# One load of x per sequence in place of two: three input tiles that become the result, the norm's four pieces and the bias add spread out, and the transposes of the sum put ahead of those of the heads

## The reference

```python
qk = x @ W_attn + b_attn                  # q, k; the values are x itself
y = _causal_attn(q, k, v)                 # first attention
e = v[:, :, 1:, :] - y[:, :, :-1, :]
k2 = x[:, :-1] @ W_k2 + b_k2
y2 = _causal_attn(q2, k2, e)              # second attention, on e
...
return proj(y) + proj(y2)                 # = (y + y2) @ W_proj + 2 b_proj
...
x = _layernorm(x + attn(x))               # for every sequence
x = _layernorm(x + ffn(x))                # ffn touches sequence 0 alone
```

## Time and profile before

| | |
|---|---|
| time, median of 3 runs | 2399.45 us (2398.83 to 2400.66) |
| the profiled execution's own time | 2397.73 us |
| its span in the profile | 2395.9 us |
| TensorE busy | 2311.0 us, 96% |
| VectorE / ScalarE / GpSimd busy | 2076.4 (87%) / 1788.7 (75%) / 1552.9 us (65%) |
| granted TensorE clock, mean | 0.987 |
| DMA, mean | 105 GB/s, queues busy 54.3% |
| HBM read / written | 74.60 MB / 16.78 MB |

### The profile page before, as it was taken

One profiled execution on the slowest core, in us unless ns is written; L12 is line 12 of the kernel. 1 busy time (PEld: TensorE's weight loads), 2 busy tenths in 40 slices (PEclk: granted clock), 3 DMA queues, 4 the chain that ended last, 5 costly groups with the idle time before them and its releaser, 6 DMA issues.

```text
span 2395.9 us, 64955 instructions
## 1 busy us (share of the span) xinstructions
PE 2311.0 (96%) x19670; PEld 1324.6 (55%) x19670; DVE 2076.4 (87%) x9178; ACT 1788.7 (75%) x3456; POOL 1552.9 (65%) x2439
## 2 busy tenths in 40 slices
PE   6999999999999999999999999999999999999997
PEld 4555555555555555555555555555555555555454
DVE  5889998998998989989998899998988999998555
ACT  3677777787877777777777787877777777777653
POOL 4466666766766676676666766766676676666432
PEclk9799999999999999999999999999999999999999
DMA  7455555655656556565655656555565565655111
GB/s 122 90 109 109 104 96 101 122 114 114 113 104 109 96 112 119 110 119 109 113 95 99 124 113 114 113 104 109 99 109 116 111 120 109 112 97 89 55 56 59
DMA packets 187749, 250.83 MB, mean 105 GB/s; under 512 B 26760, under 2 KB 103184, under 8 KB 187408
## 3 DMA queue, kind: packets, MB, share of 16 engines
q1 hardware_dynamic: 186448, 245.10, 54.3%
q10 hardware_dynamic: 960, 1.57, 0.5%
HBM read 74.60 MB, written 16.78 MB: 38 GB/s over the span
## 4 chain that ended last, share of the span: by engine, by line
PE 71%; ACT 12%; POOL 6%; issue 5%; DMA 2%; SPq 2%; DVE 1%; ACTq 0%; POOLq 0%; DVEq 0%
PE out_t L668 21%; PE score_t L707 18%; PE misc L759 10%; PE score L718 8%; PE out_t L733 6%; ACT heads_t L589 5%; ACT prob L563 5%; PE misc L801 4%; POOL prob L451 2%; PE score L859 2%; SPq L385 2%; DMA stack_q<-neg_l 2%; ACT resid L287 1%; PE misc L785 1%; PE score L875 1%
## 5 line engine op out<-in xcount | busy, mean ns | idle before, releaser
L923 DVE CUSTOM_DVE_ANT_0 junk<-score,mask_rows 128x384 bf16<-128x384 f32 (+3 forms) x3584 | 1682.2, 515 | 227.5 <-PE score L718 219.1
L563 ACT ACTIVATE prob<-score_t 128x512 f32<-128x512 f32 x2560 | 1368.5, 599 | 262.9 <-PE score_t L707 261.1
L451 POOL TENSOR_SCALAR_AFFINE_SELECT prob<-prob 128x512 f32<-128x512 f32 (+1 forms) x1280 | 712.3, 561 | 648.2 <-ACT prob L563 638.4
L707 PE MATMUL score_t<-stack_q,stack_k 50*128 50x128 f32 (+5 forms) x4096 | 982.2, 359 | 19.7 <-DMA stack_q<-neg_l 6.7
L718 PE MATMUL score<-stack_k,stack_q 48*128 48x512 f32 (+3 forms) x4096 | 982.0, 348 | 2.7 <-DVE max_cols L923 1.2
L707 PEld LDWEIGHTS score_t<-stack_q,stack_k 50*128 50x128 f32 (+1 forms) x4096 | 611.5, 186 | 556.5 <-ACT prob L563 304.8
L668 PE MATMUL out_t<-prob,value 128*17 128x512 f32 (+3 forms) x8192 | 657.4, 439 | 0.0
L718 PEld LDWEIGHTS score<-stack_k,stack_q 48*128 48x128 f32 x4096 | 618.1, 188 | 24.5 <-DVE max_cols L923 9.7
L923 DVE DVE_READ_ACCUMULATOR2_ANT max_cols<- 128x1 f32 x4096 | 339.5, 83 | 0.0
L668 PEld LDWEIGHTS out_t<-prob,value 128*17 128x17 f32 x8192 | 184.5, 97 | 211.7 <-issue 130.7
L479 POOL TENSOR_TENSOR part_l<-part_f,part_h 128x512 fp32r<-128x512 f32 x192 | 245.7, 1280 | 16.3
(11 more groups left out here) (100 smaller groups left out, 1727.0 us busy)
## 6 DMA issues: line engine op xcount, KB each, us to landing
stack_k<-part_h SPq DMA_DIRECT2D x512, 128.0 KB, 4.6
stack_k<-part_l SPq DMA_DIRECT2D x256, 128.0 KB, 5.1
stack_q<-part_h SPq DMA_DIRECT2D x248, 128.0 KB, 4.2
x_full<-x_turned SPq DMA_DIRECT2D x32, 512.0 KB, 13.0
x_in<-L_attn_x SPq DMA_DIRECT2D x32, 512.0 KB, 14.8
resid<-L_attn_x SPq DMA_DIRECT2D x32, 512.0 KB, 5.2
stack_q<-part_l SPq DMA_DIRECT2D x124, 128.0 KB, 5.1
layer_out<-resid SPq DMA_DIRECT2D x31, 512.0 KB, 7.9
```

The source lines that it names most:

```text
L451: e.affine_select(out=view, in_=view, compare_op=ALU.is_ge, fill=0.0, base=-unit_parts(unit)[1], pattern=[[0, runs], [0, cut], [1, P]], ch ...
L563: e.activation(prob[pair % RING][:, slot % 2 * 512:slot % 2 * 512 + 512], score_t[time % KEY_DEPTH][:, :], ACT.Exp, scale=1.0 / np.sqrt(HE ...
L707: done = e.matmul(score_t[now % KEY_DEPTH][:, col:col + n], keys[rows, pair, kb * P:(kb + 1) * P], stack_q[b % 2][rows, pair, kb * P:token ...
L923: e.tensor_tensor_reduce(junk[count % JUNK][:, 0:n], score[number % MAX_DEPTH][:, col:col + n], mask, 1.0, -3e38, ALU.add, ALU.max, max_co ...
```

## The change

x is loaded once, into `x_in[b % 3]`, at (5,5) of the sequence before (SP waits there for the store that last read this tile). The copy into `value1` moves from (5,2) to (7,2). The tile stays, takes the bias in two halves at (4,4) and (7,6) of its own sequence, then the projection, is normed in place and is stored from there. The load of `resid` at (2,2) with its wait is gone. The four pieces of the norm go from (0,7), (0,9), (1,1), (1,3) to (0,8), (3,1), (3,6), (4,4), and the store from (1,5) to (4,7). Sequence 0 is now stored like the others and read back into `x1_routed`, which lies over `x_full`. On PE the block that turns `y_sum` stands ahead of the transposes of the heads.

```diff
 USUAL = {"proj": ((3, 7), (6, 7)), "added": ((4, 0), (7, 0)), "stats": ((5, 5), (6, 4), (7, 5), (8, 1)),
-         "var": ((8, 3),), "guess": ((8, 4),), "refine": ((8, 5),), "apply": ((8, 7), (8, 9), (9, 1), (9, 3)), "store": ((9, 5),)}
+         "var": ((8, 3),), "guess": ((8, 4),), "refine": ((8, 5),), "apply": ((8, 8), (11, 1), (11, 6), (12, 4)), "store": ((12, 7),)}
...
-        x_in = sb("x_in", [P, blocks, width])
+        x_in = [sb(f"x_in{i}", [P, blocks, width]) for i in range(3)]
         x_next = sb("x_next", [P, blocks, width])
-        resid = sb("resid", [P, blocks, width])
...
+        x_full_at = nc.sbuf_base
         x_full = sb("x_full", [P, halves, tokens])
...
+        x1_routed = nc.alloc_sbuf_tensor_at("x1_routed", [P, blocks, width], F32, offset=x_full_at)
...
-                    if b + 1 < batches:
-                        e.wait_ge(s_value1, b + 1)
-                        e.dma_start(x_in[:, :, :], x[b + 1].rearrange("(t p) c -> p t c", p=P)).then_inc(s_x, 16)
...
-                b = ahead - 1
-                if (place, slot) == (2, 2) and 0 <= b < batches:
-                    if b == 1:
-                        e.wait_ge(s_apply, blocks)
-                    elif b > 1:
-                        e.wait_ge(s_out, 16 * (b - 1))
-                    e.dma_start(resid[:, :, :], x[b].rearrange("(t p) c -> p t c", p=P)).then_inc(s_resid, 16)
...
+                b = ahead + 1
+                if (place, slot) == (5, 5) and 2 <= b < batches:
+                    if b >= 3:
+                        e.wait_ge(s_out, 16 * (b - 2))
+                    e.dma_start(x_in[b % 3][:, :, :], x[b].rearrange("(t p) c -> p t c", p=P)).then_inc(s_x, 16)
...
+                if time == SLOTS * (last_batch + 1):
+                    e.wait_ge(s_xsplit, 2 * halves * batches)
+                    e.wait_ge(s_out, 16)
+                    e.dma_start(x1_routed[:, :, :], out[0].rearrange("(t p) c -> p t c", p=P)).then_inc(s_x1, 16)
...
-                if (place, slot) == (3, 6) and 0 <= ahead - 1 < batches:
-                    wide = bass.AP(bias2[:, :].tensor, bias2[:, :].offset, [list(bias2[:, :].ap[0]), [0, blocks], [1, width]])
...
-                    e.tensor_tensor(resid[:, :, :], resid[:, :, :], wide, ALU.add).then_inc(s_biased, 1)
+                for half in range(2):
+                    if (place, slot) == ((4, 4), (7, 6))[half] and 0 <= ahead < batches:
+                        rows2 = x_in[ahead % 3][:, 2 * half:2 * half + 2, :]
...
+                        e.tensor_tensor(rows2, rows2, wide, ALU.add).then_inc(s_biased, 1)
...
-                if (place, slot) == (5, 2) and 0 <= ahead + 1 < batches:
+                if (place, slot) == (7, 2) and 0 <= ahead + 1 < batches:
...
-                    apply_norm(e, b, t, x1_routed if b == 0 else resid, resid)
+                    apply_norm(e, b, t, x_in[b % 3], x_in[b % 3])
...
+                b = ahead - 1
+                if 0 <= b < batches:
+                    for hf in range(halves):
+                        if (place, slot) == ((1, 4), (2, 4))[hf]:
+                            e.wait_ge(s_full, min(N_PIECES * (b + 2) + 2 + hf, N_PIECES * batches))
+                            if hf == 0:
+                                e.wait_ge(s_added, GROUPS * (b + 1))
+                            else:
+                                e.wait_ge(s_yt, halves * b + 1)
+                            for t in range(blocks):
+                                done = e.transpose(misc[:, t * P:(t + 1) * P], y_sum[b % 2][:, t, hf * P:(hf + 1) * P], ident[:, :])
+                            done.then_inc(s_yt_pe, 1)
+
+
                 if slot == 4 and 0 <= unit - 1 < end:
                     e.wait_ge(s_heads, unit)
```

More of the change, by code:

```diff
@@ L150, in build_layer @@
         misc = ps("misc", 512)
-        s_wq, s_wk2, s_wproj, s_next, s_resid, s_out = (sem(f"s_{n}") for n in ("wq", "wk2", "wproj", "next", "resid", "out"))
-        s_x, s_xt = sem("s_x"), sem("s_xt")
+        s_wq, s_wk2, s_wproj, s_next, s_out = (sem(f"s_{n}") for n in ("wq", "wk2", "wproj", "next", "out"))
+        s_x, s_xt, s_x1 = sem("s_x"), sem("s_xt"), sem("s_x1")
         s_stack = {(kind, hf): sem(f"s_stack_{kind}{hf}") for kind in ("q", "k", "k2") for hf in range(halves)}
@@ L372, in _ @@
                     if piece[3] == N_PIECES // 3:
-                        e.dma_start(x_in[:, :, :], x[0].rearrange("(t p) c -> p t c", p=P)).then_inc(s_x, 16)
+                        e.dma_start(x_in[0][:, :, :], x[0].rearrange("(t p) c -> p t c", p=P)).then_inc(s_x, 16)
                         e.dma_start(wp[:, :, :], w_proj.rearrange("(h p) n -> p h n", p=P)).then_inc(s_wproj, 16)
                         e.dma_start(bias2[:, :], b_proj.rearrange("(o n) -> o n", o=1).to_broadcast([P, width])).then_inc(s_wproj, 16)
+                if piece and piece[3] == N_PIECES:
+                    e.dma_start(x_in[1][:, :, :], x[1].rearrange("(t p) c -> p t c", p=P)).then_inc(s_x, 16)
+                b = ahead + 1
[3 more added lines that the diff above has]
+                    e.dma_start(x_in[b % 3][:, :, :], x[b].rearrange("(t p) c -> p t c", p=P)).then_inc(s_x, 16)
                 for a, b in ((0, ahead + 1), (1, ahead)):
@@ L388, in _ @@
                 now_due = due("store", time)
-                if now_due and now_due[0]:
+                if now_due:
                     b = now_due[0]
                     e.wait_ge(s_apply, blocks * (b + 1))
-                    e.dma_start(out[b].rearrange("(t p) c -> p t c", p=P), resid[:, :, :]).then_inc(s_out, 16)
+                    e.dma_start(out[b].rearrange("(t p) c -> p t c", p=P), x_in[b % 3][:, :, :]).then_inc(s_out, 16)
+                if time == SLOTS * (last_batch + 1):
+                    e.wait_ge(s_xsplit, 2 * halves * batches)
+                    e.wait_ge(s_out, 16)
+                    e.dma_start(x1_routed[:, :, :], out[0].rearrange("(t p) c -> p t c", p=P)).then_inc(s_x1, 16)
                 if step_at.get(time) == LOADS:
@@ L452, in _ @@
                                     pattern=[[0, runs], [0, cut], [1, P]], channel_multiplier=-1).then_inc(s_mask, 1)
[L454 to L459 removed]
+                for half in range(2):
+                    if (place, slot) == ((4, 4), (7, 6))[half] and 0 <= ahead < batches:
+                        rows2 = x_in[ahead % 3][:, 2 * half:2 * half + 2, :]
+                        wide = bass.AP(bias2[:, :].tensor, bias2[:, :].offset, [list(bias2[:, :].ap[0]), [0, 2], [1, width]])
+                        e.wait_ge(s_value1, ahead + 1)
+                        if ahead == 0:
+                            e.wait_ge(s_bias, 1)
+                        e.tensor_tensor(rows2, rows2, wide, ALU.add).then_inc(s_biased, 1)
                 for a, b in ((0, ahead + 1), (1, ahead)):
@@ L503, in _ @@
                     e.tensor_copy(value1[:, :, :, 0:HEAD_DIM],
-                                  x_in[:, :, :].rearrange("p t (h d) -> p t h d", d=HEAD_DIM)).then_inc(s_value1, 1)
+                                  x_in[b % 3][:, :, :].rearrange("p t (h d) -> p t h d", d=HEAD_DIM)).then_inc(s_value1, 1)
                 done = unit - 2
@@ L773, in _ @@
                                     ident[:, :]).then_inc(s_neg_pe, 1)
[L775 to L786, removed]
                 now_due = due("proj", time)
@@ L947, in _ @@
                     b, pair = now_due
-                    rows2 = resid[:, 2 * pair:2 * pair + 2, :]
+                    rows2 = x_in[b % 3][:, 2 * pair:2 * pair + 2, :]
                     e.wait_ge(s_proj, 2 * b + pair + 1)
-                    if pair == 0:
-                        e.wait_ge(s_biased, b + 1)
+                    e.wait_ge(s_biased, 2 * b + pair + 1)
                     e.tensor_tensor(rows2, misc[:, :].rearrange("p (t c) -> p t c", t=2), rows2, ALU.add).then_inc(s_attended, 1)
@@ L957, in _ @@
                         e.wait_ge(s_attended, 2 * b + t // 2 + 1)
-                    take_stats(e, b, t, resid)
+                    take_stats(e, b, t, x_in[b % 3])
                     if t == last:
```

5 lines of the change are left out of this document (2 added, 3 removed).

## The result

The changed kernel takes 2382.23 us (median of 5 runs, 2375.94 to 2386.96) against a median of 2399.45. The ratio on record is 0.9942, with a 95% interval of 0.9925 to 0.9959; it is not the quotient of these two medians, which is 0.9928 and lies inside the interval. Predicted were 2387.0 us, a range of 2375 to 2403, and "a little faster". The profiled execution took 2386.96 us, with a span of 2385.2 (before: 2395.9).

A forecast was written before the change was run, and what follows sets the result against it. PE nearly always busy; only a few places longer than their fixed lengths, the longest at the norm's pieces. Terms -3.0 - 5.3 + 0.3 + 0.6 - 4 - 1 = -12.4 us: 2387.0 against 2399.45, range 2375 to 2403.

The forecast's parts named there:

- Part 1: Norm out of units 0 and 1: exponential of (0,9) ends 0.46 us earlier, PE's scores of (1,3) likewise.
- 0.73 by itself: Unit 1: the norm's move alone would start the heads' transposes 0.73 us earlier in 30 sequences, 22 us.
- Part 2, unit 1: `y_sum` turned first at (1,4): PE idles 0.8 us for POOL's add, only 0.10 left, -3.0 us over 30 sequences.
- Part 2, unit 2: `y_sum` turned first at (2,4), heads ready meanwhile: -0.17 us in each of 31 sequences, -5.3 us.
- Part 3: Norm's pieces on ACT: +0.02 us each at (3,1), +0.6 us; nothing at (3,6) and (4,4).
- Part 4: POOL in unit 7 takes the copy and a half add, with 0.6 us to spare before (7,9): cost nothing.
- rival 2: Slower: x late for the copy at (7,2), POOL leaves unit 7 late; 2420 at 16.8 us landing; chance 0.11.
- Part 5: 31 loads of 512 KB gone, SP no longer held by `resid`'s load, shortening PE's wait for the maxima's DMAs: -4 us.
- Part 6: POOL's bias add leaves the tail, -2.1 us; its halves in the last sequence cost +1.1; sum -1.
- rival 4: Both halves of the bias add meet a multiply in the last sequence: 2.4 us instead of 1.1, 2388.3; chance 0.06.

## Why the prediction was right, point by point

- **What bounds it, Part 1.** Right. The exponential of (0,9) came 0.5 us behind the norm's piece, and the scores of (1,3) are reached 0.47 earlier (0.46 said). Putting the norm back costs 13 us. The "0.73 by itself" holds only once the add is early (0.75); with the late add the old order of PE gives 0.47.
- **Part 2, unit 1.** Right in mechanism and size: PE idles 0.8 us for POOL's add, 30 times; 0.10 left was said, 0.04 to 0.07 is there. The semaphore took 0.15 us, not my 0.06 estimated from ACT to PE; that is most of the difference. Over 28 sequences unit 1 gave 1 to 2 us, not 3.
- **Part 2, unit 2.** -0.17 said, -0.16 measured.
- **Part 3.** +0.02 said; from slot 0 to slot 9 of unit 3 PE's scores start as far apart after as before, to 0.01 us: nothing.
- **Part 4.** Nothing, right; the slack was 0.74 (0.6 said). The load lands after 6.0 us, so rival 2 had no ground.
- **Part 5.** -4 said; -0.20 + 0.07 in 28 sequences is -3.6. The place is right, the reason half: SP's lateness alone won nothing back, it takes the load.
- **Part 6.** -1 was said for the tail and the last sequence together, as -2.1 and +1.1. Measured are -1.4 and +1.25, so -0.2, and each of the two is near its term by luck. In the tail the multiply of 2.81 us is gone, and with it more than the 2.1 said: from the multiply of the earlier trace rows at 2351.80 to the last one at 2381.00 it was 29.20 us, after 25.39 (2342.58 to 2367.97), -3.8, of which some 1.7 is not the multiply. And the end is 2.4 us longer, which no step had. These 1.7 and 2.4 come from TensorE's clock, next section. In the last sequence the +1.1 did not come: no multiply met a half add, and their durations are those of before. What made it 1.25 us longer is not shown; its granted clock was 0.93 in the mean, and 0.95 before. So rival 4 did not come either. The rule of the Trainium skill on the shared port ("SBUF — State Buffer", "Who interferes with whom") is borne out by the earlier trace rows. It is borne out a second time by a multiply that both kernels have: it takes 1.20 us instead of 0.69 beside POOL's add into `y_sum` (after: multiply at 2319.35, add of 0.73 at 2319.27). In both cases the multiply ends 0.55 us behind POOL's instruction.
- **The sum.** The forecast was 2387.0 on a sum of -12.4; the spans differ by -10.7 and the medians by 17.2 (interval of the ratio: 10 to 18 us). The medians favour the changed kernel by more than the profiled executions do; why is not shown.

## What to carry to other kernels

A waiting instruction hands its gain to the next one in line: before moving work off an engine, work out who is next at that place and when its input is ready, to a tenth of a us. Here 0.73 us per sequence became 0.04, since the next wait (an add behind two casts) stood right there, and swapping it won 25 us, more than the change itself. Which of two orders is shorter depends on that: `y_sum` first cost 0.26 us a sequence in the kernel before, and saved 0.28 once the norm was moved and the add early.

## What the runs showed of the hardware that was not expected

TensorE's granted clock falls in the tail behind an idle PE, and differs from one profiled execution to the next where the code is the same. The windows view of PE at the end, after (window, us, PE busy, granted clock, DMA share, GB/s): the last two groups of eight matmuls fall into windows of 0.74 and 0.50; 0.50 is the lower level, 1.2 GHz.

```profile
2360.00:2368.00 8.00, 4.92 (x19) 1.00 0.00 0
2368.00:2372.00 4.00, 2.60 (x8) 0.74 0.00 0
2372.00:2376.20 4.20, 3.78 (x8) 0.50 0.37 125
```

The same groups before, at the full clock:

```profile
2381.00:2384.00 3.00, 1.99 (x8) 1.00 0.01 3
2384.00:2387.00 3.00, 1.99 (x8) 1.00 0.35 119
```

In both kernels PE had been idle 3.8 us in front of the first group. 2.60 + 3.78 against twice 1.99 is the 2.4 us. The kernel before paid at another place: behind the blocked multiply PE was idle 2.2 us, and the next 3.1 us ran at 0.62. That is the 1.7 us above: its four matmuls and the eight behind them took 3.23 and 2.39 us, where the same groups take 1.88 and 1.89 at the full clock.

```profile
2355.20:2358.30 3.10, 2.97 (x4) 0.62 0.04 8
```

Of the ten experiments only the kernel before with `y_sum` first kept the full clock in both groups (1.99, 1.99), with the same idle of 3.8 us in front; the early add on the kernel before had 3.78 twice, 3.6 us more than the kernel before, which it partly made up since it did not fall behind the blocked multiply: its tail is 1.9 us longer. In the last sequence of the changed kernel, 2252 to 2256 ran at 0.50, and that sequence was 1.25 us longer.

The largest such difference stands at the start, and no long idle goes with it. Sequences 0 and 1 together take 140.6 to 141.4 us in five of the twelve profiled executions (before and after among them), 137.4 to 137.6 in three and 135.4 to 135.8 in four. In both kernels below PE is idle once in the first window, for 0.79 us, and for at most 0.43 us in the second. The changed kernel:

```profile
94.00:103.50 9.50, 8.71 (x80) 1.00 0.38 47
103.50:110.30 6.80, 6.78 (x42) 0.50 0.76 116
```

The changed kernel with the heads first:

```profile
94.00:103.50 9.50, 8.64 (x79) 1.00 0.33 42
103.50:110.30 6.80, 6.37 (x65) 1.00 0.78 118
```

The same again from 130.8 to 137.6 (0.50 and 1.00). So the spans of two single executions can differ by 5 to 6 us before the third sequence starts, as much as the step from the changed kernel to the one with the heads first is worth. The mean over sequences 2 to 29 leaves start and tail out, so the sizes above do not depend on this. Each of these is one profiled execution; what decides the clock was not tried.
